# Expert stage: spread weights for four row blocks at once into four PSUM banks, sum and moments placed between the fours

## The reference

```
router_probs = softmax(x @ router_w + router_b)        # 8 experts
top_p, top_i = top_k(router_probs, 2)                  # the two best
top_p = top_p / sum(top_p)
expert_out = einsum('bnd,edc->bnec', x, expert_w) + expert_b
out = einsum('bnk,bnkc->bnc', top_p, gathered experts)
t = t + out
```

## Time and profile before

| what | value |
|---|---|
| timed runs | 2306.16, 2308.48, 2319.19 us |
| the profiled execution | 2298.41 us, span 2296.6 us |
| mean granted clock of TensorE | 0.913 |
| PE busy over the span | 1752.8 us (76%) |
| DVE busy | 1584.8 us (69%) |
| ACT busy | 1142.8 us (50%) |
| POOL busy | 1168.2 us (51%) |
| first and last sum of the expert stage | 1782.1 and 2291.8 us |

### The profile page before, as it was taken

How to read it: one execution, slowest core, us unless ns; L and a number is a source line. 1 busy time by engine, 2 the same in 40 slices (tenths; PEclk the granted TensorE clock), 3 DMA queues, 4 the chain that set the end, 5 groups by cost and what they waited for, 6 DMA issues and landing times. The chain is left out here.

```text
span 2296.6 us, 44402 instructions
## 1 busy us (share of the span) xinstructions
PE 1752.8 (76%) x11740; PEld 1164.1 (51%) x11740; DVE 1584.8 (69%) x5005; ACT 1142.8 (50%) x2610; POOL 1168.2 (51%) x1594
## 2 busy tenths in 40 slices
PE   5778748888646659838887737978746999999998
PEld 3444437778522238724444426877734444444443
DVE  6888704566757768838787730665664889889887
ACT  5898813333125549817676633333216545555541
POOL 5777604676857740026566520766765343444330
PEclk9999979999779989959999979999885999999999
DMA  3777547888633314958789746988764555555552
GB/s 115 204 193 190 156 137 240 273 297 284 209 117 93 95 51 82 191 179 242 233 252 267 217 115 179 311 276 272 260 193 144 155 157 158 155 158 160 153 140 68
DMA packets 475473, 423.19 MB, mean 184 GB/s; under 512 B 224690, under 2 KB 372402, under 8 KB 475314
## 3 DMA queue, kind: packets, MB, share of 16 engines
q1 hardware_dynamic: 402610, 303.87, 47.4%
q10 hardware_dynamic: 72704, 117.47, 15.2%
HBM read 236.68 MB, written 150.99 MB: 169 GB/s over the span
## 5 line engine op out<-in xcount | busy, mean ns | idle before, releaser
L699 PE MATMUL cp_pv<-cp_weight,cp_zt 64*128 64x320 f32 x2048 | 369.8, 469 | 103.4 <-ACT cp_zt L637 87.8
L257 POOL TENSOR_TENSOR cc_ln_rstd<-cc_ln_var,numbers 128x8 f32<-128x8 f32 x128 | 255.5, 1996 | 188.5 <-DVE cc_ln_var L248 179.6
L523 DVE SCALAR_TENSOR_TENSOR a_res<-cp_pv,cp_mask,cp_sig 128x64 f32<-128x64 f32 x1024 | 263.9, 322 | 123.9 <-ACT cp_sig L646 119.4
L1537 DVE TENSOR_TENSOR ex_xe<-ex_spread,ex_xd 128x512 f32<-128x512 f32 x512 | 322.6, 683 | 36.0 <-PE ex_spread L1779 35.8
L829 PE MATMUL cc_sum<-a_res,cc_bch 128*128 (+1 forms) x2048 | 297.9, 296 | 62.6 <-DMA cc_bch<-b_scratch 59.3
L919 ACT ACTIVATE cc_p<-cc_sum 128x512 f32 (+1 forms) x128 | 135.8, 1061 | 376.4 <-PE cc_sum L829 239.7
L829 PEld LDWEIGHTS cc_sum<-a_res,cc_bch 128*128 128x128 f32 x2048 | 269.8, 205 | 85.0 <-issue 76.1
L646 ACT ACTIVATE cp_sig<-cp_pv 128x384 f32<-128x384 f32 x512 | 249.7, 493 | 125.7 <-PE cp_pv L699 124.0
L699 PEld LDWEIGHTS cp_pv<-cp_weight,cp_zt 64*128 64x128 f32 x2048 | 184.3, 189 | 222.3 <-issue 193.7
L1796 PE MATMUL ex_po<-ex_xe,ex_expert 128*64 128x512 f32 x1024 | 267.8, 647 | 0.1
L1589 POOL TENSOR_TENSOR ex_rstd<-ex_var,numbers 128x8 f32<-128x8 f32 x64 | 104.7, 1636 | 270.4 <-DVE ex_var L1485 260.5
(11 more groups left out here) (186 smaller groups left out, 2976.4 us busy)
## 6 DMA issues: line engine op xcount, KB each, us to landing
cc_bch<-b_scratch SPq DMA_DIRECT2D x256, 256.0 KB, 3.9
gate_scratch<-cp_sig SPq DMA_DIRECT2D x128, 256.0 KB, 2.6
b_scratch<-cp_b_stage SPq DMA_DIRECT2D x128, 256.0 KB, 4.0
cc_g<-gate_scratch ACTq DMA_DIRECT2D x128, 256.0 KB, 4.5
after_conv<-cc_p ACTq DMA_DIRECT2D x128, 256.0 KB, 3.8
ex_xd<-ex_xt SPq DMA_DIRECT2D x256, 128.0 KB, 2.5
cp_x<-in_x SPq DMA_DIRECT2D x64, 256.0 KB, 3.3
cc_p<-in_x ACTq DMA_DIRECT2D x64, 256.0 KB, 3.6
```

The costliest lines, as they stand in the source:

```text
L257: pool.tensor_tensor(rstd[q][:], var[q][:], numbers[:, 0:1].to_broadcast([P, tiles]), ALU.pow).then_inc(scaled if shifts else known, 1)
L523: dve.scalar_tensor_tensor(a_res[:, h, :, row], bank[:, h, 3 * C:4 * C], mask_sb[:, h, row:row + 1], sig[u.mod(2)][:, 0, h, i, :], ALU.mul ...
L699: pe.matmul(pv[slot(u, i)][:, h, 0:COLS], zt[u.mod(2)][half, i * P:(i + 1) * P], weight[half, :], start=True, stop=True).then_inc(v_made, 1)
L1537: dve.tensor_tensor(xe[u.mod(2)][:, :, h, i * P:(i + 1) * P], pb[2 * (p % 2) + h][:].rearrange("p (e t) -> p e t", e=EP), xd[u.mod(8)][:, ...
```

## The change

- `spread_out(u, g)` now fills four banks at once: for a four g of blocks it has 16 matmuls in the order expert pair outside, bank inside, so that successive matmuls use the four different groups of 32 partitions and the four banks. A table FOURS gives the half and the row block of each. It is called twice a step instead of four times, and waits until DVE has read all four banks of the four before. Each bank has its own semaphore.
- DVE multiplies the four blocks of a four after each other. Between the two fours stand the sum of unit s-2 and the first routing piece (or the split); after the second four stand the moments and the second routing piece. The moments are those of unit s+11 instead of s+10, behind the second four instead of between.
- Statistics, variances, scales and shifts have four buffers instead of two, loaded inputs eight instead of four; loads run one step earlier (s+13), the residual's load one step later (s).
- ACT normalises in two halves, one before `take` and one after it (after the routing's sigmoids in turn 2), and stores unit s-3 instead of s-2, behind the outputs' copy.
- PE's order is: half of the expert sum, flip, second spread, other half, rate, first spread of the next unit, turned outputs.
- Steps run from -13 to 66, with 16 written out ahead of the loop.

```diff
@@ -1352,17 +1352,17 @@
-        xs = [m.sb(f"x{q}", [P, H, R, C]) for q in range(4)]
+        xs = [m.sb(f"x{q}", [P, H, R, C]) for q in range(8)]
-        stats = [m.sb(f"stats{q}", [P, T, 3]) for q in range(2)]
-        var = [m.sb(f"var{q}", [P, T]) for q in range(2)]
-        rstd = [m.sb(f"rstd{q}", [P, T]) for q in range(2)]
-        lift = [m.sb(f"lift{q}", [P, T]) for q in range(2)]
+        stats = [m.sb(f"stats{q}", [P, T, 3]) for q in range(4)]
+        var = [m.sb(f"var{q}", [P, T]) for q in range(4)]
+        rstd = [m.sb(f"rstd{q}", [P, T]) for q in range(4)]
+        lift = [m.sb(f"lift{q}", [P, T]) for q in range(4)]
@@ -1405,7 +1405,7 @@
-        x_in = [m.sem(f"x_in{q}") for q in range(4)]
+        x_in = [m.sem(f"x_in{q}") for q in range(8)]
@@ -1413,13 +1413,14 @@
...
             m.sem(n) for n in ("ranked", "weighed", "share_made", "w_made", "w_turned", "w_copied", "w_split"))
-        spread_a, spread_b, xe_dve = (
-            m.sem(n) for n in ("spread_a", "spread_b", "xe_dve"))
+        spread_made = [m.sem(f"spread_made{q}") for q in range(4)]
+        xe_made = m.sem("xe_made")
         e_made, y_copied, y_turned, out_made, seen = (
...
         RANK_STEPS, WEIGH_STEPS = 8, 6
-        DVE_BLOCKS = 8
-        FIRST, LAST, HEAD, TAIL = -12, G + 1, 14, 16
+        BLOCKS = R * H
+        FOURS = [[(0, 0), (1, 1), (0, 2), (1, 3)], [(1, 0), (0, 1), (1, 2), (0, 3)]]
+        FIRST, LAST, HEAD, TAIL = -13, G + 2, 16, 16
...
@@ -1437,9 +1438,9 @@
...
                         return
-                    if (u - 4).real:
-                        sp.wait_ge(xn_made, u.n - 3)
-                    sp.dma_start(xs[u.mod(4)][:], x[:, :, row_block(u), :]).then_inc(x_in[u.mod(4)], 16)
+                    if (u - 8).real:
+                        sp.wait_ge(xn_made, u.n - 7)
+                    sp.dma_start(xs[u.mod(8)][:], x[:, :, row_block(u), :]).then_inc(x_in[u.mod(8)], 16)
...
@@ -1454,7 +1455,7 @@
...
                         sp.sem_inc(seen, 1)
-                        sp.wait_ge(xe_dve, (u.n - 7) * DVE_BLOCKS)
+                        sp.wait_ge(xe_made, (u.n - 7) * BLOCKS)
                         sp.sem_inc(seen, 1)
...
@@ -1462,28 +1463,29 @@
...
                 def step(s):
-                    load(s + 12)
+                    load(s + 13)
                     double(s + 7)
-                    load_rest(s + 1)
+                    load_rest(s)
...
             def _(dve):
-                def measure(u):
-                    if not u.real:
-                        return
-                    q = u.mod(2)
-                    if (u - 2).real:
-                        dve.wait_ge(multiplied, u.n - 1)
-                    dve.wait_ge(x_in[u.mod(4)], u.div(4) * 16 + 16)
-                    for i in range(R):
-                        ins = dve.bn_stats(stats[q][:, i * H:(i + 1) * H, :].rearrange("p t s -> p (t s)"),
-                                           xs[u.mod(4)][:, :, i, :].rearrange("p h c -> p c h"))
-                    ins.then_inc(counted, 1)
-                    dve.wait_ge(counted, u.n + 1)
-                    dve.tensor_scalar(var[q][:], stats[q][:, :, 2], 1.0 / C, 1e-5, ALU.mult, ALU.add
-                                      ).then_inc(var_made, 1)
+                def measure(u, part):
+                    if not u.real:
+                        return
+                    q = u.mod(4)
+                    if part == 0:
+                        if (u - 4).real:
+                            dve.wait_ge(multiplied, u.n - 3)
+                        dve.wait_ge(x_in[u.mod(8)], u.div(8) * 16 + 16)
+                    for i in (2 * part, 2 * part + 1):
+                        dve.bn_stats(stats[q][:, i * H:(i + 1) * H, :].rearrange("p t s -> p (t s)"),
+                                     xs[u.mod(8)][:, :, i, :].rearrange("p h c -> p c h")).then_inc(counted, 1)
+                    if part == 1:
+                        dve.wait_ge(counted, (u.n + 1) * R)
+                        dve.tensor_scalar(var[q][:], stats[q][:, :, 2], 1.0 / C, 1e-5, ALU.mult, ALU.add
+                                          ).then_inc(var_made, 1)
...
@@ -1525,19 +1527,19 @@
...
-                def scale_inputs(u, p, h):
-                    if not u.real:
-                        return
-                    i = (p + h) % R
-                    if p == 0 and h == 0:
+                def scale_inputs(u, g, k):
+                    if not u.real:
+                        return
+                    h, i = FOURS[g][k]
+                    if g == 0 and k == 0:
                         dve.wait_ge(doubled[u.mod(8)], u.div(8) * (16 * H * 2) + 16 * H * 2)
...
                             dve.wait_ge(e_made, (u.n - 1) * H)
-                    dve.wait_ge(spread_b if h else spread_a, u.n * R + p + 1)
+                    dve.wait_ge(spread_made[k], u.n * 2 + g + 1)
                     dve.tensor_tensor(xe[u.mod(2)][:, :, h, i * P:(i + 1) * P],
-                                      pb[2 * (p % 2) + h][:].rearrange("p (e t) -> p e t", e=EP),
+                                      pb[k][:].rearrange("p (e t) -> p e t", e=EP),
                                       xd[u.mod(8)][:, h, i * P:(i + 1) * P].unsqueeze(1).to_broadcast([P, EP, P]),
-                                      ALU.mult).then_inc(xe_dve, 1)
+                                      ALU.mult).then_inc(xe_made, 1)
...
@@ -1553,22 +1555,19 @@
...
                     four = s + 4 - turn
-                    scale_inputs(s, 0, 0)
-                    scale_inputs(s, 0, 1)
+                    for k in range(4):
+                        scale_inputs(s, 0, k)
                     finish(s - 2)
-                    scale_inputs(s, 1, 0)
-                    scale_inputs(s, 1, 1)
-                    measure(s + 10)
                     if turn == 0:
...
                         split_shares(s + 1)
-                    scale_inputs(s, 2, 0)
-                    scale_inputs(s, 2, 1)
-                    scale_inputs(s, 3, 0)
-                    scale_inputs(s, 3, 1)
+                    for k in range(4):
+                        scale_inputs(s, 1, k)
+                    measure(s + 11, 0)
+                    measure(s + 11, 1)
                     if turn == 0:
...
@@ -1582,10 +1581,10 @@
-                    q = u.mod(2)
+                    q = u.mod(4)
-                    if (u - 2).real:
-                        pool.wait_ge(xn_made, u.n - 1)
+                    if (u - 4).real:
+                        pool.wait_ge(xn_made, u.n - 3)
@@ -1643,23 +1642,26 @@
...
                         weigh(four, 3)
+
                 run(pool, step)
...
             def _(act):
-                def normalise(u):
-                    if not u.real:
-                        return
-                    q = u.mod(2)
-                    act.wait_ge(known, u.n + 1)
-                    if (u - 2).real:
-                        act.wait_ge(xt_made, u.n - 1)
-                    for i in range(R):
+                def normalise(u, part):
+                    if not u.real:
+                        return
+                    q = u.mod(4)
+                    if part == 0:
+                        act.wait_ge(known, u.n + 1)
+                        if (u - 2).real:
+                            act.wait_ge(xt_made, u.n - 1)
+                    for i in (2 * part, 2 * part + 1):
                         for h in range(H):
                             t = i * H + h
-                            ins = act.activation(xn[q][:, i, h, :], xs[u.mod(4)][:, h, i, :], ACT.Identity,
+                            ins = act.activation(xn[u.mod(2)][:, i, h, :], xs[u.mod(8)][:, h, i, :], ACT.Identity,
                                                  scale=rstd[q][:, t:t + 1], bias=lift[q][:, t:t + 1])
-                    ins.then_inc(xn_made, 1)
+                    if part == 1:
+                        ins.then_inc(xn_made, 1)
...
@@ -1714,12 +1716,13 @@
...
                         take_shares(s + 1)
+                    normalise(s + 9, 0)
                     take(s + 8)
-                    normalise(s + 9)
-                    store(s - 2)
                     if turn == 2:
                         weigh(s + 2)
+                    normalise(s + 9, 1)
                     take_outputs(s - 1)
+                    store(s - 3)
                     take_logits(s + 8)
...
@@ -1762,31 +1765,29 @@
...
-                def spread_out(u, p):
-
-                    if not u.real:
-                        return
-                    if p == 0:
+                def spread_out(u, g):
+
+                    if not u.real:
+                        return
+                    if g == 0:
                         pe.wait_ge(w_split, u.div(4) + 1)
                         pe.sem_inc(seen, 1)
-                    if p >= 2 or (u - 1).real:
-                        pe.wait_ge(xe_dve, u.n * DVE_BLOCKS + 2 * p - 2)
+                    if g or (u - 1).real:
```

(21 more changed lines are left out.)

## The result

Before, the median was 2307.32 us (2304.51 to 2319.19, 4 runs); after, it is 2250.34 us (2248.07 to 2252.02, 4 runs). The profiled execution took 2252.02 us (span 2249.5), 46.4 less than the profiled one of before; the stages ahead, whose code did not change, ended 11.7 us later in it (the expert stage begins at 1723.7, before at 1712.0), so the stage is compared by its own stretches.

What follows compares the result with a forecast made beforehand. Neither engine was full: PE and DVE waited for each other at hand-overs in the expert stage. Steps -32, start -3 and tail -2 made -37 us, from 2308.5 to 2271 us, range 2254 to 2296.

Steps and rivals of the forecast that it cites:

- The spread: Expert stage, PE: sixteen matmuls in four row groups take 0.33 us until the next, as eight did; 0.66 us less a step.
- The step: Middle stretch: four steps take 29.6 us instead of 31.99, DVE becomes the bound; -32 us over 54 steps.
- The clock: Middle stretch: the price of half clock stays as before, 19 us; at worst 27, +8.
- nothing of the clock's price left over: Lower end of the range: the half-clock price in the stretch vanishes, with start -5, giving 2254 us.
- The wait for shares: PE's 0.79 us wait for the shares goes, because the moments come one step earlier.
- The list of a step: Turn-by-turn timing of PE and DVE after the change: 6.60, 8.47, 7.40 and 7.15 us, 29.6 for four steps.
- Start and tail: Start: normalisations 3.99 us apart instead of 4.44, -3 (0 to -5). Tail: last steps 6.12 apart instead of 6.36, -2.
- Pairs only: Rival, chance 0.18: only two row groups run at once, a four's spread costs 0.55 us; -0.36 a step, 2286 us.
- The hand-over not hidden: Rival, chance 0.10: PE reaches the second spread late, 0.5 us left in each step; -10, 2298 us.
- A lower clock: Rival, chance 0.05: more row groups and fewer pauses on PE lower the stage's clock; at 0.78, +9, 2318 us.

Runs made afterwards that it cites:

- e9: The kernel before with rating moved between the two halves of the expert sum on PE; 2291.63 us, ratio 0.995.
- e1: The new kernel with one more 128x512 multiplication on DVE a step (0.60 us), so that PE pauses longer; 2280.84 us, ratio 0.9906.
- e5: e1 with the first two matmuls of each expert sum issued twice (0.47 us more on PE a step); 2285.85 us, ratio 0.9915.
- e13: e1 with PE's four transposes of normalised rows (flip) issued twice, filling part of the pause; 2287.26 us, ratio 0.9911.
- e2: The new kernel with the sixteen spread matmuls ordered bank by bank; 2247.29 us, ratio 0.973.
- e4: The new kernel with the sixteen spread matmuls ordered two banks at a time; 2246.99 us, ratio 0.9747.
- e8: The new kernel with the sum moved from between the fours to behind the second four; 2258.39 us, ratio 0.979.
- e10: The new kernel with flip moved ahead of the first half of the expert sum; 2245.79 us, ratio 0.9744.
- e6: The kernel before with the first two matmuls of each expert sum issued twice; 2318.7 us, ratio 1.0041.
- e14: e7 with rating moved between the two halves of the expert sum on PE; 2338.6 us, ratio 1.0137.
- e7: The new kernel with spreads of two banks at a time, four times a step, and PE's order of before; 2288.36 us, ratio 0.9941.
- e3: The kernel before with the four transposes of turned outputs issued twice; 2312.29 us, ratio 1.0028.
- e11: The new kernel with ACT's old order: take, the whole normalisation, then the routing's sigmoids; 2274.83 us, ratio 0.9861.
- e12: The new kernel with sixteen steps in the loop's body instead of eight; 2255.66 us, ratio 0.9779.

## Why the prediction was wrong

**The spread, right.** Sixteen in 0.40 us, 0.33 until the next (1969.14 to 1969.47), as forecast. By the estimate from the Trainium skill's page TensorE: Matmul & The Clock Gate (Part 3: Packing small matmuls) the 0.33 would have been 0.45; the trace doesn't agree, and the measurement decides.

**The step, right.** Forecast 29.6 us for four, measured 29.70: DVE is the bound, PE waits for it in turns 1 and 2, the hand-over to the second four is hidden behind the sum. The loop's pause of 0.56 was not in the list; the fours of steps that hold it take 30.14. Over 54 steps: -31.2 for -32.

**The clock, the step that failed.** The prediction put it: "I take the price as before, 19; at worst 27, +8." It measured 0, so 19.5 us of the 21.8 by which the stage fell short of the sum (58.8 for 37) are here. The working asked how much lateness PE has room for once the clock is at half; it never asked whether PE's new row of work would still make it fall. The change parted the two halves of the expert sum by flip and a spread, and by rating, a spread and the turned outputs, and no pause is over 1.2 us. e9 shows that rating between the halves takes 10 of 12 drops from the old kernel; e1, e5 and e13 show that longer pauses bring drops into the new one and that work in them takes the drops away. One of the drops before, by windows and by PE's order:

```profile
2104.66:2108.07 3.41, 2.23 (x28) 1.75 (x28) 3.15 (x8) 0.82 (x2) 1.87 (x4) 1.00 0.62 165
2108.07:2111.48 3.41, 3.31 (x16) 1.62 (x18) 3.34 (x10) 1.62 (x5) 0.84 (x2) 0.50 0.56 142
```

```profile
2102.71 1.94 PE L1796 MATMUL ex_po<-ex_xe,ex_expert 128*64 128x512 f32 x8
...
2108.17 0.61 PE L1779 MATMUL ex_spread<-ex_wt,ex_select 32*128 32x128 f16 x8 [1.29 <-DVE ex_xe L1537]
2108.71 1.11 PE L1738 MATMUL ex_tp<-ident,ex_xn 128*128 128x128 f32 x4
2109.76 2.77 PE L1796 MATMUL ex_po<-ex_xe,ex_expert 128*64 128x512 f32 x8
```

Over all kernels the traces give, for the stretch, the longest time at full clock without a matmul of the expert sum (pauses included), PE's longest pause, and the drops:

| kernel | without the sum, us | pause, us | drops |
|---|---|---|---|
| after, e2, e4 | 2.4 | 1.2 | 0 |
| e5 | 2.4 | 1.0 | 0 |
| e8 | 2.5 | 1.6 | 0 |
| e13 | 2.8 | 1.4 | 0 |
| e1 | 2.8 | 1.8 | 6 |
| e10 | 2.9 | 1.4 | 0 |
| e9 | 3.3 | 1.0 | 2 |
| e6 | 3.7 | 0.4 | 6 |
| e14 | 4.0 | 1.7 | 20 |
| e7 | 4.2 | 1.0 | 17 |
| before | 4.5 | 1.3 | 12 |
| e3 | 4.5 | 0.9 | 13 |
| e11 | 4.7 | 1.6 | 4 |

(e12 is as the new kernel, save its two loop turns.) The pause alone doesn't sort them: 1.6 us went without a drop in e8, 0.4 with six in e6. The first column does better in whether there are drops, though not in how many, and e1 is its exception. Most of these kernels differ in more than this. The clean pairs are e9 against before, where PE's order alone changes, and e13 against e1, where a pause is filled and the first column stays. So it is shown that PE's order can take most drops away and that the length of a pause counts; what the clock falls on exactly stays open.

That the price could vanish stood in the range ("nothing of the clock's price left over", start -5), as its lower end. Worked out, these two give 2308.5-32-5-2-19.6 = 2250, and not the 2254 that the prediction wrote: the end was set 4 us above its own terms. The measured median is 2250.34.

**The wait for shares, right that it goes, wrong in why.** "One step earlier it is there before": e11 has the moments a step earlier and waits 18.8 us. It was ACT's new order, with the normalisation split around take, for which the prediction had "nothing in the steady part" because ACT has 17 us of work in 32. Busy share says nothing of an instruction's place in its queue: a whole normalisation ahead of the shares holds POOL and PE up. The new order is worth 27 us there, some 20 of them outside the clock if each of the 4 drops cost 19.5/12 = 1.6, more if they cost e1's 0.4. The list of a step took ACT to be on time for no cost; that it was on time was the doing of an edit priced at nothing, so this part of the step's forecast was lucky.

**Start and tail.** -4.2 for -3: the period is 4.00 as forecast (3.99). -3.9 for -2, and mostly for other reasons: the last steps are 6.19 apart (2220.62 to 2226.81), forecast 6.12, before 6.36, but one of them took 6.74, so they give 0.4 in all. A further 1.1 is one more drop of the clock that the kernel before had, at 2241.2, and 2.4 stands near the end, where two sums are 3.92 us apart instead of 6.30. The last was not followed up.

**The rivals.** Pairs only: refuted, since sixteen run in 0.40, and in 0.44 even in e2. The hand-over not hidden: refuted, 1.8 us in all; e8 shows what it would have been without the sum between. A lower clock: the opposite happened.

## What to carry to other kernels

Where a clock drop recurs in a steady loop, count its price as a term of its own and ask of each reordering what it does to the pauses and to the spacing of the large matmuls; here it was worth nearly two thirds of the step gain. Widening the hand-over from two buffers to four hid its own latency, and PE had room for an order with parted halves; with pairs of banks, parting them cost 48 us in e14 over e7 and saved 8 in e9 over before, so such a move is to be measured in its own kernel. And before an edit of an engine's order is priced at nothing, follow who waits for each instruction behind it, however idle the engine.

## What the runs showed of the hardware

- Matmuls in different row groups don't wait for each other's turn: sixteen written bank by bank, one row group each, took 0.44 us, interleaved 0.40. A further matmul of a group comes 0.06 behind the one ahead, so by estimate one group after another they would have taken 15 x 0.06+0.21 = 1.1.
- Four row groups cost as much as two: sixteen in 0.40 us, eight in 0.40.
- Most drops of the clock in the stretch lasted 3.41 us, some 6.83, and one 17.07 (e14). Each began inside a pause of PE or at most 1.5 us behind one, of 0.4 to 5.1 us. Pauses as long passed without a drop (1.6 us in e8).
- A drop cost 1.6 us on average in the kernel before, where PE was late, and 0.4 in e1, where it had room.
- A loop turn cost 0.56 us on DVE with eight steps in the body and 4.75 with sixteen (e12).
